# A two-layer language-model tower: masked attention turned before its exponential, and projections split into parts behind the turn

## The reference, cut to what matters

```
h  = token_map(ids)                       # (2, 1024, 1024)
q, k, v = norm(h) @ Wq, norm(h) @ Wk, norm(h) @ Wv ; q, k turned by rope
s  = q k^T / sqrt(32), causal
first layer:   p = softmax(s)
second layer:  p = softmax(s where s >= 128th largest of its row, else -1e18)
h  = h + (p v) @ Wo ;  h = h + mixture(norm(h))
```

## Time and profile before

| what | us |
|---|---|
| median of 3 runs | 5141.41 (5139.87 to 5142.2) |
| the profiled execution | 5140.53 |
| its span | 5138.7 |
| PE busy / DVE busy / ACT busy | 3749.4 / 3507.8 / 3167.7 |

### The profile page before, as it was taken

How to read it: one execution, slowest core, us unless ns; L and a number is a source line. 1 busy time by engine, 2 the same in 40 slices (tenths; PEclk the granted TensorE clock), 3 DMA queues, 4 the chain that set the end, 5 groups by cost and what they waited for, 6 DMA issues and landing times. The chain is left out here.

```text
span 5138.7 us, 79699 instructions
## 1 busy us (share of the span) xinstructions
PE 3749.4 (73%) x23338; PEld 2207.5 (43%) x23480; DVE 3507.8 (68%) x10383; ACT 3167.7 (62%) x7058; POOL 289.1 (6%) x213
## 2 busy tenths in 40 slices
PE   6998999999999999924555355555555555554799
PEld 2445766666444444412333233333333333332454
DVE  3564777776333356558888888888888888887444
ACT  1123777776000011169999599999999999999200
POOL 2332000000000023300000000000000000000000
PEclk8999999999999999966766676666766767766899
DMA  4235323232111123310011011111011110110222
GB/s 150 64 70 157 78 54 79 57 76 94 57 49 49 49 49 76 77 37 10 17 27 26 1 26 26 26 23 25 6 26 26 24 25 6 24 26 6 79 86 78
DMA packets 276875, 249.81 MB, mean 49 GB/s; under 512 B 170048, under 2 KB 209232, under 8 KB 276432
## 3 DMA queue, kind: packets, MB, share of 16 engines
q1 hardware_dynamic: 275888, 245.13, 18.1%
q0 software_dynamic: 544, 0.07, 0.0%
HBM read 167.56 MB, written 77.59 MB: 48 GB/s over the span
## 5 line engine op out<-in xcount | busy, mean ns | idle before, releaser
L1036 ACT ACTIVATE a_sign<-a_x,a_state 128x384 fp8e4<-128x384 f32 (+5 forms) x1536 | 1343.0, 876 | 124.4 <-DVE a_state L1172 85.7
L942 PE MATMUL a_ps_s<-k,q 128*128 128x512 bf16 (+3 forms) x1474 | 500.1, 484 | 689.5 <-DVE a_x L1273 660.0
L953 PE MATMUL a_ps_t<-ident,arena 128*128 128x128 f32 x2304 | 484.8, 355 | 193.9 <-ACT a_invT L1005 130.1
L942 PEld LDWEIGHTS a_ps_s<-k,q 128*128 128x128 bf16 x1536 | 167.4, 130 | 914.6 <-DVE a_x L1273 748.3
L971 PE MATMUL a_ps_o<-a_probT,vals 128*32 128x128 f32 x4608 | 407.4, 327 | 184.8 <-ACT a_probT L1001 184.4
L953 PEld LDWEIGHTS a_ps_t<-ident,arena 128*128 128x128 f32 x2304 | 338.4, 179 | 332.8 <-ACT a_invT L1005 142.9
L727 ACT ACTIVATE a_prob<-a_x_neg,a_shift 128x640 f32<-128x640 f32 (+7 forms) x512 | 397.1, 776 | 79.4 <-DVE a_x_neg L770 61.2
L1273 DVE TENSOR_SCALAR_CACHE_REDUCE a_x<-a_ps_s 128x128 f32<-128x128 f32 (+7 forms) x512 | 383.7, 754 | 85.4 <-PE a_ps_s L945 60.4
L1001 ACT COPY a_probT<-a_ps_t 128x512 f32<-128x512 f32 (+3 forms) x768 | 346.6, 476 | 111.1 <-PE a_ps_t L953 110.1
L770 DVE TENSOR_SCALAR_CACHE_REDUCE a_x_neg<-a_ps_s 128x640 f32<-128x640 f32 (+7 forms) x512 | 378.8, 751 | 38.4 <-PE a_ps_s L651 25.4
L971 PEld LDWEIGHTS a_ps_o<-a_probT,vals 128*32 128x32 f32 x4608 | 269.2, 128 | 294.4 <-ACT a_probT L1001 268.2
(11 more groups left out here) (229 smaller groups left out, 5941.4 us busy)
## 6 DMA issues: line engine op xcount, KB each, us to landing
q<-qk SPq DMA_DIRECT2D x256, 256.0 KB, 4.8
qk<-p_qkT SPq DMA_DIRECT2D x32, 960.0 KB, 6.2
h_rows<-h SPq DMA_DIRECT2D x32, 512.0 KB, 6.9
k<-qk SPq DMA_DIRECT2D x256, 64.0 KB, 5.1
h<-tok_h SPq DMA_DIRECT2D x16, 512.0 KB, 4.0
arena<-in_wo SPq DMA_DIRECT2D x16, 512.0 KB, 9.0
o<-a_o SPq DMA_DIRECT2D x16, 512.0 KB, 2.7
q<-o SPq DMA_DIRECT2D x16, 512.0 KB, 5.6
```

Source lines behind the costliest of these rows:

```text
L942: nc.tensor.matmul(ps_s[:, n % 2, a:a + w], q[:, y, head, i * P:(i + 1) * P], k[:, y, a:a + w], start=(y == 0), stop=False, skip_group_che ...
L953: mm = nc.tensor.transpose(ps_t[:, (n + 1) % 3, c:c + P], prob[:, par, at:at + P], ident[:, :])
L1036: ins = nc.scalar.activation(to, x[:, par, at:at + w], ACT.Sign, scale=-1.0, saturate=False, bias=state[:, par, 0, n:n + 1], accum_out=sta ...
```

## The change

**Second attention.** `prob`, the exponentials on ScalarE, `keep`, `normalise`, `invert` and the transposed inverse go away. Instead:

- `mark` writes a bf16 mask on VectorE (one `tensor_scalar`: -1e18 where the score is under the limit), 14 per slot in the places of the keeps;
- `turn` builds the shifted and masked scores of a chunk in PSUM: the fp32 transposes of the raw scores `xs`, one bf16 matmul that adds minus the row maximum (as three bf16 parts that lie in 48 rows), and, except in the first tile, one bf16 matmul of mask times identity for each block;
- `evac` is now an `Exp` activation out of PSUM instead of a copy;
- the row maxima are split in `start`, transposed once per slot by TensorE (`turn_top`) and copied by ScalarE (`top_evac`, after its pass 2);
- the values are widened by 32 columns of ones, so that `values` also gives the row sums, and its result takes two PSUM banks; for that the ring of transposes has two banks, not three;
- `output` copies 1024 columns out of PSUM; outputs and sums go to memory undivided, with four stores per pair instead of two;
- scores lie in a ring of three buffers, and the hardware loop holds six slots and runs four times.

**Last mixture.** Each tile also loads the sums (four DMAs, each over 32 partitions), and VectorE takes their reciprocal (128x1024) and multiplies (`scale_rows(j + 2)`, ahead of `residual(j + 1)`). The first tile is scaled at the end of the attention (`scale_first`). `out_project` waits for the scaled tile.

**Projections.** TensorE transposes the fp32 rows (10 blocks), ScalarE copies them to bf16 (`hi`), VectorE subtracts (`rest`), ScalarE copies to bf16 (`mid`), VectorE subtracts again (`lo`). GpSimd has nothing left to do there.

The diff, cut to its core:

```diff
 def project(...):
+        ps_qk = ps("ps_qk", [P, 3, BANK])
+        TURNS = chunks(QK)
                 def qk_transposes(j, par):
-                    pe.wait_ge(parts_ready, j + 1)
                     if not (isinstance(j, int) and j == 0):
-                        pe.wait_ge(qkT_ready, j * NQ)
+                        pe.wait_ge(rest_ready, j * NQ)
                     for t, (a, n) in enumerate(TURNS):
+                        pe.wait_ge(rope_done, j * 3 + (t + 1))
                         for c in range(0, n, P):
+                            m = nc.tensor.transpose(ps_qk[:, t, c:c + P], rot[:, par, a + c:a + c + P], ident[:, :])
                 def qk_evac(j, par):
                     for t, (a, n) in enumerate(TURNS):
                         act.wait_ge(qkT_done, j * NQ + (t + 1))
+                        nc.scalar.copy(qkT[:, par, a:a + n], ps_qk[:, t, 0:n]).then_inc(hi_ready, 1)
+                    for t, (a, n) in enumerate(TURNS):
+                        act.wait_ge(rest_ready, j * NQ + (t + 1))
+                        nc.scalar.copy(qkT[:, par, QK + a:QK + a + n], rest[:, a:a + n]).then_inc(mid_ready, 1)
-            @block.gpsimd
...
                 def step(j, par, first, last):
+                    if split:
+                        rests(j - 2, par)
                     if not last:
                         norm(j + 1, 1 - par)
+                    if split:
+                        lows(j - 2, par)
                     for n in range(3):
                         rotate(j, par, n)
 def kept_attention(...):
                     def turn(n, m, i, a, w):
+                        to = ps_t[:, (n + 1) % 2, 0:w]
+                        pe.wait_ge(probT_ready, (s - 2) * TURNED + max(n, 1))
                         for c in range(0, w, P):
+                            nc.tensor.matmul(to[:, c:c + P], xs[old][:, at:at + P], ident[:, :], start=(c == 0), stop=False,
+                                             is_transpose=True, skip_group_check=True)
+                        mm = nc.tensor.matmul(to.rearrange("p (b c) -> p b c", c=P), row_of[:, m * TT + i, :],
+                                              topT[:, :].unsqueeze(1).to_broadcast([SPLITS * 2 * TT, w // P, P]),
+                                              start=False, stop=(i == 0), skip_group_check=True)
+                        for c in range(0, w if i else 0, P):
+                            mm = nc.tensor.matmul(to[:, c:c + P], mask[:, at:at + P], ident_b[:, :], start=False,
+                                                  stop=True, skip_group_check=True)
                     def evac(n, m, i, a, w):
                         act.wait_ge(turn_done, (s - 2) * TURNED + (n + 2))
+                        nc.scalar.activation(probT[:, n % 4, 0:w], ps_t[:, (n + 1) % 2, 0:w], ACT.Exp).then_inc(probT_ready, 1)
+                    def mark(r):
+                        return nc.vector.tensor_scalar(mask[:, at:at + w], old_x[:, at:at + w], limit[:, r:r + 1], MASKED,
+                                                       ALU.is_lt, ALU.mult)
+                    def output():
+                        nc.vector.tensor_copy(o[:, :], ps_o[:, :]).then_inc(o_ready, 1)
+                    def scale_first():
+                        dve.wait_ge(first_in, 16 * (1 + G))
+                        scale(nc, dve, first_o, first_total[:, :]).then_inc(first_scaled, 1)
+def scale(nc, dve, o, total):
+    nc.vector.reciprocal(total, total)
+    dve.drain()
+    return nc.vector.tensor_tensor(o, o, total, ALU.mult)
 def last_mixture(...):
+                def scale_rows(j):
+                    dve.wait_ge(o_in[j % RING], both_landed(j))
+                    scale(nc, dve, o[:, j % RING, :], totals[:, j % RING, :]).then_inc(scaled, 1)
+                scale_rows(1)
                 residual(0)
                 for j in range(NT):
+                    if j + 2 < NT:
+                        scale_rows(j + 2)
                     if j + 1 < NT:
                         residual(j + 1)
```

279 lines of the change are left out of this document (133 added, 146 removed).

## The result

The changed kernel takes 5241.91 us in the median of 4 runs (5234.26 to 5243.34) against 5140.64 for the kernel before in the same session: ratio 1.0194, 95% interval 1.0176 to 1.0211. It is 101 us slower where 140 us less were forecast. The profiled execution has a span of 5239.3 us, against 5138.7 before.

What follows compares the result with a forecast made beforehand. Three engines share the bound: VectorE's queue in passes 2 to 4, TensorE's in 0 and 1. Slots -105 and -4, loop jumps -15, attention's end +8, last mixture +10, projections -34: -140, median 5001 us, range 4940 to 5120.

Steps and rivals of the forecast that it cites:

- The four loads of sums: Last mixture: four loads per tile on SP's queue, 2 us of issue in 18, ring of four tiles; cost nothing unless VectorE lags.
- the VectorE bound of 19.1: Last mixture: with 9.6 us of scaling VectorE needs 19.1 us a tile against TensorE's 18.3, so it becomes the bound.
- The rule of the reciprocal: Scaling by the sums: the skill's repeat count of 8 at 0.96 GHz, an estimated 8.5 us for 1024 columns.
- Passes 0 and 1, 35.1 us: Second attention's slot, up to ScalarE's first Sign of pass 2: 35.1 us, three quarters at TensorE's upper level; before 34.8.
- the 38 that I had named: Sign for the slot: the prediction is wrong if passes 0 and 1 exceed 38 us.
- a busier TensorE rises sooner: Passes 0 and 1: TensorE, busy 27 of 31 us with shorter gaps, should reach its upper clock level sooner.
- rival 1: Copies behind each pass: TensorE keeps falling to the lower clock level; slot 77.2, 5103 us, chance 0.20.
- Rival 2: Passes 0 and 1: TensorE becomes the bound through two-bank ping-pong, 42.5 us, 5223 in all; chance 0.13, table loads included.
- Pass 2's 12.9: Slot of the second attention: VectorE's share falls under ScalarE's 10.6 us, so pass 2 takes 12.9 us instead of 14.3.
- The end of the attention, +8: Behind the last slot: last values alone on TensorE and first tile's scaling, less masks and inverse; +8 us (0 to 13).
- The projections, -34: Projections: fp32 transposes shorten TensorE's tiles by 25 us, the chain behind the last tile by 9; -34 us (-42 to 0).
- rivals 1 and 3: The first has its own line; the other: mark at the keep's pace per column, slot 76.4, 5076 us, chance 0.08.

## Why the prediction was wrong

**The four loads of sums, "nothing, unless VectorE lags".** This step failed, and cost 132 of the 241 us between forecast and result. I counted the ring's depth from TensorE's use of a tile, as it was before. The change puts VectorE's `scale_rows(j + 2)` in front of that use, at the head of a turn, while the loads of that tile are still issued by the end of the turn before. The lead fell from a whole tile to 2 us, and the landing time of 12 us came into the loop. The forecast had even listed what is queued at SP, but not asked when each load is issued and when it is first waited for. With the lead restored the tile is 18.29 us; the VectorE bound of 19.1 that I had put there did not come, because reciprocal and product take 7.8 us and not 9.6: 17.3 by the same sum.

**The rule of the reciprocal.** The Trainium skill (VectorE: DVE Perf Modes, the walkthrough's hardware budget) led to an estimate of 8.5 us for 1024 columns. The trace has 6.55, or 6.4 ns per column. The slope of the two short reciprocals was too steep as well, at 8.0.

**Passes 0 and 1, 35.1 us.** Measured 38.4 in the mean, from the end of a slot's first instruction to the first Sign of pass 2 as the forecast counted: at its upper bound of 38.5, and over the 38 that I had named as the point where the prediction fails. The step that failed is that TensorE's 27 us, at the upper level for three quarters, stay under ScalarE's 31, so that the lower level costs something in the copies behind a pass alone; its ground was "a busier TensorE rises sooner". The chain is at 0.60 in pass 0 although TensorE is busy 15.0 of 15.8 us, later than before and not sooner, and the added 48-row matmul is what holds the level. ScalarE waits for TensorE already among the Signs: the two rounds of Signs with their copies take 28.2 us where 26.2 were put, the copies behind pass 0 6.3 where 4.7 were put, those behind pass 1 4.0 for 3.0, and these two stretches ran at 0.99 and 1.00. They are long because TensorE is behind from pass 0. With the padding the same count is 35.1 us, which is the forecast: the work and its pace at the upper level were sized rightly, and the clock was not.

What rival 1 said came true in its size (slot 77.2 forecast, 77.3 measured), though its mechanism, the lower level in the copies behind a pass, was not the one. Rival 2's ping-pong did not show: two banks alone cost nothing. Its 5223 us lie near the measured 5242 by chance, for the slots gave 77.3 us and not 81, and the rest came from the last mixture, which it does not mention.

**The other parts of the slot.** The mark takes 0.73 us for 1024 columns, under the expected 0.75 to 0.82. Pass 3 went from 13.95 to 12.9 us, and the part behind it from 16.5 to 15.1, as forecast. Pass 2's 12.9 did not come (14.5), because ScalarE enters it late: pass 1's last copies wait for TensorE. So 2.4 us a slot were won on VectorE, and 1.7 of them lost again on TensorE's side. An ordinary slot before is 77.4 without a jump and 79.0 with one, and the mean fell from 78.1 to 77.3. Ten jumps fewer at 1.6 us each would be 16 of the 23 us that the 29 slots gained.

**The end of the attention, +8.** Measured +21.6. VectorE waits 36.8 us for the last pair's values where it waited 21.9; I had 9 less 4.2 for the masks and 2 for the inverse. Here too the chain starts at the lower level:

```profile
4741.00:4760.00 19.00, 18.62 (x129) 11.20 (x130) 0.32 (x1) 5.25 (x12) 0.00 (x0) 0.69 0.68 225
4760.00:4779.00 19.00, 18.11 (x184) 11.98 (x181) 0.84 (x1) 6.53 (x12) 0.00 (x0) 1.00 0.13 51
```

The masks have one buffer, so the last marks also waited 9.6 us for the turning of the pair before. With the padding this stretch is 139.8 us, close to the 137.4 of before.

**The projections, -34.** Right: -37 by itself.

**The range.** It took in rivals 1 and 3 but put the loads at nothing on both sides. A bound from the landing time, 12 us a tile as the changed kernel shows it, would have been 180 us.

## What to carry to other kernels

A ring's depth says nothing by itself. Write down for each load the instruction behind which it is issued and the first instruction that waits for it; when a step is put in front of the old consumer, that distance shrinks, even with the ring unchanged. And before TensorE is given more work because it has room, look at the granted clock of that stretch and at how many rows each new matmul feeds: in this kernel a matmul of 48 rows held the clock at its lower level for some 7 us more in each slot, and padding it to 128 rows with zeros gave back 2% of the whole time.

## What the runs showed of the hardware

- The granted clock does not follow TensorE's busy share alone. With TensorE busy 5.00 of each 5.00 us in the stretches shown, the clock rose 12 us behind the start of the chain with the 48-row matmul (8 to 18 over 27 slots), 5 us with the same matmul on 128 rows, 80 of them zeros (3 to 8), and 5 us with none (3 to 7).
- While TensorE ran twenty fp32 transposes and nothing else, the granted clock rose from 0.50 to 1.00, and the chain behind them lost it again with TensorE busy.
- A matmul over 48 rows is as long as one over 128, to 0.03 us at 256 columns (0.39 and 0.42 us at the lower level).
- Less work can lower the clock so far that nothing is gained: without the masks 8.6 us of TensorE's work a slot went, and 0.2 us of the slot (77.32 to 77.15), with slots of 79.3 and 74.3 us in turn.
- The reciprocal of 128x1024 fp32 takes 6.55 us, to within 2 ns in 15 of 15.
- Four loads that spread one row of sums over 32 partitions each, in pieces of 512 bytes, land in 5.3 to 12.8 us. With several such groups under way, issuing one group holds the queue for up to 9.5 us where it takes 2.6 otherwise.
